# Transposes of a mixture-of-experts stage moved from TensorE to transposing DMAs on the SyncE queue

## The reference, cut to what matters

```
xn = rms_norm(layernorm(x))
scores = einsum('bsd,ed->bse', xn, w_router)          # 8 experts
ids = top 2 of scores; c = softmax(scores) at ids
h = einsum('bsd,ehd->bseh', xn, w_up)                 # 2 * 704 columns
val, gate = split(h, 2);  h = val * silu(gate)        # 704
y = einsum('bseh,edh->bsed', h, w_down)               # back to 256
out = sum over the 2 chosen experts of y * c, + xn input (skip)
```

## Time and profile before

| | us |
|---|---|
| three runs, median (lowest to highest) | 480.11 (479.94 to 484.15) |
| profiled execution, its own time | 481.64 |
| span of its one core | 479.8 |
| TensorE busy | 389.6 (81%) |
| VectorE busy | 278.7 (58%) |
| ScalarE busy | 260.5 (54%) |
| GpSimd busy | 196.5 (41%) |

### The profile page before, as it was taken

One profiled execution on the slowest core, in us unless ns is written; L12 is line 12 of the kernel. 1 busy time (PEld: TensorE's weight loads), 2 busy tenths in 40 slices (PEclk: granted clock), 3 DMA queues, 4 the chain that ended last, 5 costly groups with the idle time before them and its releaser, 6 DMA issues.

```text
span 479.8 us, 10289 instructions
## 1 busy us (share of the span) xinstructions
PE 389.6 (81%) x2600; PEld 272.6 (57%) x2601; DVE 278.7 (58%) x704; ACT 260.5 (54%) x473; POOL 196.5 (41%) x186
## 2 busy tenths in 40 slices
PE   1898897899984411059999999999999999999980
PEld 1676686788774311025666666666666666666660
DVE  4787677888883779854444444454444444444540
ACT  2898856745466750654555555555545555455530
POOL 2534535667774422112333344343344333344221
PEclk9999999799996555569999999999999999999997
DMA  7967991222261124001212222222222212222221
GB/s 250 376 244 252 382 313 48 66 68 67 66 216 46 45 59 122 23 14 32 46 36 44 44 44 33 41 38 44 44 44 33 43 35 44 44 44 33 35 24 11
DMA packets 24645, 41.93 MB, mean 87 GB/s; under 512 B 5040, under 2 KB 20400, under 8 KB 23600
## 3 DMA queue, kind: packets, MB, share of 16 engines
q1 hardware_dynamic: 17088, 31.17, 19.4%
q0 software_dynamic: 7536, 10.52, 13.8%
HBM read 32.17 MB, written 9.50 MB: 87 GB/s over the span
## 4 chain that ended last, share of the span: by engine, by line
PE 66%; DMA 10%; DVE 9%; ACT 5%; issue 4%; POOL 2%; SPq 2%; ACTq 0%; DVEq 0%; POOLq 0%
PE bank L1232 30%; DMA expert_w<-in_wup 6%; PE bank L1253 5%; PE bank L1283 4%; PE bank L1282 4%; PE bank L1284 4%; PE bank L1119 3%; DVE expert_w L931 3%; PE bank L1171 3%; DMA arena<-in_ctxT 2%; ACT arena L435 2%; PE bank L1180 2%; PE bank L1152 2%; PE bank L1264 2%; PE bank L1286 2%
## 5 line engine op out<-in xcount | busy, mean ns | idle before, releaser
L1232 PE MATMUL bank<-expert_w,arena 128*128 x702 | 160.4, 366 | 11.4 <-ACT arena L627 11.4
L741 POOL DMA_INDIRECT out<-arena,add_idx x39 | 61.7, 1581 | 115.9 <-ACT arena L608 115.9
L1232 PEld LDWEIGHTS bank<-expert_w,arena 128*128 128x128 f16 x702 | 62.9, 99 | 65.4 <-issue 14.8
L1051 DVE SCALAR_TENSOR_TENSOR arena<-bank,dn_small,arena 128x512 f32<-128x512 f32 x78 | 45.3, 581 | 39.2 <-PE bank L1232 24.0
L731 POOL DMA_INDIRECT arena<-xrow_hbm,take_idx x39 | 38.7, 993 | 67.5 <-PE bank L1264 46.2
L1282 PE MATMUL bank<-expert_w,arena 128*128 x195 | 53.2, 273 | 0.9 <-DVE arena L1035 0.9
L1283 PE MATMUL bank<-expert_w,arena 128*128 x195 | 53.2, 273 | 0.0
L1284 PE MATMUL bank<-expert_w,arena 128*128 x195 | 53.2, 273 | 0.0
L1035 DVE COPY arena<-bank 128x1024 f16<-128x1024 f16 x39 | 27.0, 691 | 42.3 <-PE bank L1253 42.3
L627 ACT ACTIVATE arena<-bank 128x512 f16<-128x512 f16 x39 | 23.3, 596 | 39.6 <-PE bank L1264 39.6
L1057 DVE TENSOR_TENSOR arena<-arena 128x512 f16<-128x512 f32 x39 | 27.0, 692 | 27.1 <-ACT arena L633 27.1
(11 more groups left out here) (181 smaller groups left out, 740.1 us busy)
## 6 DMA issues: line engine op xcount, KB each, us to landing
expert_w<-in_wup SPq DMA_DIRECT2D x8, 1408.0 KB, 7.3
expert_w<-in_wdn SPq DMA_DIRECT2D x10, 640.0 KB, 9.1
rows<-in_x SPq DMA_DIRECT2D x8, 256.0 KB, 6.8
arena<-in_ctxT SPq DMA_DIRECT2D x8, 256.0 KB, 4.6
xrow_hbm<-front SPq DMA_DIRECT2D x8, 256.0 KB, 2.2
out<-rows SPq DMA_DIRECT2D x8, 256.0 KB, 2.5
expert_w<-in_wdn SPq DMA_DIRECT2D x20, 64.0 KB, 9.0
cst_b<-in_consts_b SPq DMA_DIRECT2D x1, 960.0 KB, 7.8
```

Source lines behind the costliest of these rows:

```text
L741: pool.indirect_dma_start(out=out, in_=yt[:, i % 2], in_offset=None, out_offset=bass.IndirectOffsetOnAxis(ap=add_idx[:, i:i + 1], axis=0), ...
L1051: V.scalar_tensor_tensor(out=hh[:, cols], in0=src, scalar=h_scale[:, ds(e, 1)], in1=sg[:, cols], op0=ALU.mult, op1=ALU.mult).then_inc(s_h, 1)
L1232: last = T.matmul(bank[q][:, 0:n], xsT[:, slot, (2 * a + c) * P:(2 * a + c + 1) * P], up_w[:, ds(w0 + c * UPC + w * 2 * H + lo, n)], start ...
```

## The change

The transposes of the gathered rows and of h leave TensorE. SyncE issues a transposing DMA from SBUF to SBUF for each: one of 4 blocks of 128x128 fp16 for the rows (128 KB) and one of 11 blocks for `hs` (352 KB), 39 times each. The PSUM banks that held transposes become a second set for the up projection (banks 0 to 2 and 3 to 5) and for y (6 and 7); `hs` and `hT` get two buffers. The down projection of a slot moves one step later (step i + 3), and GpSimd issues four takes ahead in place of five. The last down matmul runs over 128 rows in place of 64. `tile_e` and others of the small tiles move to other places of the same buffer.

```diff
+            def step_e(it, k, r):                                    # @block.sync
+                if live(r, 2, NSLOT):
+                    i, half, slot = at(it, k, 2)
+                    sp.wait_ge(s_hhi, 2 * i + 2)
+                    sp.wait_ge(s_hlo, 2 * i + 2)
+                    if r >= 4:
+                        sp.wait_ge(s_y, i - 1)
+                    sp.dma_start_transpose(hT[:, slot], hs[:, slot]).then_inc(s_hT[slot], 16)
+                if live(r, 0, NSLOT):
+                    i, half, slot = at(it, k, 0)
+                    sp.wait_ge(s_xs[slot], 16 * half + 16)
+                    if r >= 2:
+                        sp.wait_ge(s_up, 3 * i - 3)
+                    sp.dma_start_transpose(xsT[:, slot], xs[:, slot, 0:4 * P]).then_inc(s_xsT[slot], 16)
+            steps(sp, step_e, E_STEPS[0], E_STEPS[0], E_STEPS[0])
...
@@ block.scalar: silu and high part of slot r-1 first, then yt of slot r-3
-                    nc.scalar.activation(hT[:, 8:NHS], hT_bank[1], ACT.Copy).then_inc(s_hTb, 1)
...
-                    nc.scalar.activation(xsT[:, slot], rowsT_bank, ACT.Copy).then_inc(s_xsT, 1)
...
+                    nc.scalar.activation(yt[:, slot], bank[6 + slot][:, 0:D], ACT.Copy, scale=pair_scale[:, ds(i, 1)]).then_inc(s_yt, 1)
...
@@ block.gpsimd
                 if i >= 2:
-                    pool.wait_ge(s_trx, i - 1)
+                    pool.wait_ge(s_xsT[i % 2], 16 * (i // 2))
                     pool.wait_ge(s_ps, i - 1)
...
-            for i in range(5):
+            for i in range(4):
                 take(i)
...
-                if i + 5 < NSLOT:
-                    take(i + 5)
+                if i + 4 < NSLOT:
+                    take(i + 4)
...
@@ block.vector: low part of slot r-1 first, then pair_scale of slot r
-                    V.tensor_copy(hT[:, 0:8], hT_bank[0]).then_inc(s_hTa, 1)
...
@@ block.tensor
+                if live(r, 1, NSLOT):
+                    i, half, slot = at(it, k, 1)
                     w_up = pe.snap(pe.value_load(tile_e[0:1, ds(i, 1)], min_val=0, max_val=NE - 1) * (2 * UPC))
+                    pe.wait_ge(s_xsT[slot], 16 * half + 16)
+                    for q, (lo, n) in enumerate(((0, HA), (HA, HA), (2 * HA, 2 * HB))):
+                        if r >= 3 and q != 1:
+                            pe.wait_ge(s_h, 2 * i - 3 + q // 2)
...
-                    for c in range(NHS):
-                        last = T.transpose(hT_bank[c // 8][:, c % 8], hs[:, c * P:(c + 1) * P], ident16[:, :])
-                    last.then_inc(s_trh, 1)
...
-                    for n in range(4):
-                        last = T.transpose(rowsT_bank[:, n * P:(n + 1) * P], xs[:, slot, n * P:(n + 1) * P], ident16[:, :])
-                    last.then_inc(s_trx, 1)
...
+                if live(r, 3, NSLOT):
+                    i, half, slot = at(it, k, 3)
                     w_dn = pe.snap(pe.value_load(tile_e[0:1, ds(i, 1)], min_val=0, max_val=NE - 1) * (2 * DNC))
+                    pe.wait_ge(s_hT[slot], 16 * half + 16)
+                    if r >= 5:
+                        pe.wait_ge(s_yt, i - 1)
```

More of the change, by code:

```diff
@@ L310, in steps @@
                 step(t // 2, t % 2, t)
-            with eng.Fori(lo // 2, hi // 2) as it:
-                step(it, 0, lo)
-                step(it, 1, lo + 1)
+            if hi > lo:
+                with eng.Fori(lo // 2, hi // 2) as it:
+                    step(it, 0, lo)
+                    step(it, 1, lo + 1)
             for t in range(hi, n):
@@ L1029, in step_e @@
             def step_e(it, k, r):
[L1030 to L1034, removed]
-                    V.tensor_copy(hT[:, 0:8], hT_bank[0]).then_inc(s_hTa, 1)
-                if live(r, 0, NSLOT):
-                    i, half, slot = at(it, k, 0)
-                    e = dve.snap(dve.value_load(tile_e[0:1, ds(i, 1)], min_val=0, max_val=NE - 1))
[L1039 to L1046, removed]
+                if live(r, 1, NSLOT):
+                    i, half, slot = at(it, k, 1)
+                    e = dve.snap(dve.value_load(tile_e[0:1, ds(i, 1)], min_val=0, max_val=NE - 1))
+                    up = bank[3 * slot:3 * slot + 3]
+                    for q, (src, cols) in enumerate(((up[1][:, 0:HA], slice(0, HA)), (up[2][:, HB:2 * HB], slice(HA, H)))):
                         dve.wait_ge(s_sg, 2 * i + q + 1)
@@ L1228, in _ @@
             products = [(c, a, w) for c in range(2) for a, w in ((0, 0), (0, 1), (1, 0))]
[L1230 to L1235, removed]
@@ L1266, in step_e @@
[L1266 to L1269, removed]
-                    up(i, slot, w_up, 2, 2 * HA, 2 * HB)
-                if live(r, 2, NSLOT):
-                    i, _, _ = at(it, k, 2)
+                    pe.wait_ge(s_xsT[slot], 16 * half + 16)
+                    for q, (lo, n) in enumerate(((0, HA), (HA, HA), (2 * HA, 2 * HB))):
+                        if r >= 3 and q != 1:
+                            pe.wait_ge(s_h, 2 * i - 3 + q // 2)
+                        for m, (c, a, w) in enumerate(products):
+                            last = T.matmul(bank[3 * slot + q][:, 0:n], xsT[:, slot, 2 * a + c],
+                                            up_w[:, ds(w_up + c * UPC + w * 2 * H + lo, n)],
+                                            start=m == 0, stop=m == len(products) - 1)
+                        last.then_inc(s_up, 1)
@@ L1281, in step_e @@
-                    for c in range(NH - 1):
-                        T.matmul(y, hT[:, c], dn_at(w_dn, c, 0), start=c == 0, stop=False)
-                        T.matmul(y, hT[:, c], dn_at(w_dn, c, 1), start=False, stop=False)
-                        T.matmul(y, hT[:, NH if c == NH - 2 else NH + 1 + c], dn_at(w_dn, c, 0), start=False, stop=False)
-                    T.matmul(y, hT[:, NH - 1], dn_at(w_dn, NH - 1, 0), start=False, stop=False)
-                    T.matmul(y, hT[0:HLAST, NH - 1], dn_at(w_dn, NH - 1, 1, HLAST), start=False, stop=True).then_inc(s_y, 1)
+                    pe.wait_ge(s_hT[slot], 16 * half + 16)
@@ new lines, in step_e @@
+                    if r >= 5:
+                        pe.wait_ge(s_yt, i - 1)
+                    y = bank[6 + slot][:, 0:D]
+                    for c in range(NH - 1):
+                        T.matmul(y, hT[:, slot, c], dn_at(w_dn, c, 0), start=c == 0, stop=False)
+                        T.matmul(y, hT[:, slot, c], dn_at(w_dn, c, 1), start=False, stop=False)
+                        T.matmul(y, hT[:, slot, NH if c == NH - 2 else NH + 1 + c], dn_at(w_dn, c, 0), start=False, stop=False)
+                    T.matmul(y, hT[:, slot, NH - 1], dn_at(w_dn, NH - 1, 0), start=False, stop=False)
@@ L1288, in _ @@
+                    T.matmul(y, hT[:, slot, NH - 1], dn_at(w_dn, NH - 1, 1), start=False, stop=True).then_inc(s_y, 1)
             steps(pe, step_e, *E_STEPS)
```

119 lines of the change are left out of this document (42 added, 77 removed).

## The result

The changed kernel takes 546.67 us at the median of five runs (537.92 to 550.1), the kernel before 480.6 (479.94 to 484.15) beside it: slower, by a ratio of 1.124 with a 95% interval of 1.115 to 1.133. The interval rests on its two runs of 537.92 and 544.49, since the other three, with a lower granted clock on TensorE (0.858 against 0.874 in the profiled one), are set apart. The profiled execution took 537.92, 56.3 more than that of before.

The account below looks back on a forecast made before the run. TensorE bounded the kernel before; afterwards the gather loop would. y(0) at 226, 18 pairs of 11.36 + 2.5 and 6.9 put y(38) at 482.4, +14.1: 495.7 profiled, 494.2 less 1.5 to the median; range 467 to 524.

Parts of the forecast that it names:

- What bounds the kernel, and what is removed: Stage E: TensorE bounds at 6.53 us a slot; without transposes its own work is 5.56 us.
- rival 2: TensorE stays the bound in stage E: a slot costs 5.56 us, the time is 451; chance 0.09.
- The loop through the gather: From y(i) through scaling, scatter, take, gather and rows' transposing DMA to up(i+4): binds, as take(i+4) stands behind scatter(i).
- 11.36 + T: Two slots' cost in us: 5.8 of scaling, scatter, take, gather and reactions, TensorE's 5.56, and T.
- T: Transposing DMA of the rows, in the wait for up(i+4): 2.2 plus 0.3, so 2.5 us.
- the 0.3 allowed: Added to the rows' transposing DMA for contention on the 16 DMA engines, where h's 352 KB may still be moving.
- The queue of SyncE: The rows' transpose stands behind h(i+2)'s, issued about 0.8 us after y(i); rows land in SBUF at 5.5, so no delay.
- H: Time SyncE is held by issuing h's 11-block transpose; claimed to cost nothing up to some 4.7 us.
- Rival 3: Transposing DMAs are slow and SyncE's queue binds: two slots cost 20.8 us, time near 633; chance 0.15.
- The end: After the last slots: y(38) ends 6.9 us after y(36), then the last scatter follows as before.
- Rivals 1 and 2: Rival 1: same gather loop, cheap transposes of 1.1 to 1.72 us, time 469 to 480, chance 0.23; rival 2 as above.
- 18 T - 30.9: Whole kernel's difference in us over 18 pairs of slots; nothing gained or lost at T = 1.72.

Follow-up runs that it names:

- five takes: The changed kernel with five takes ahead in place of four, h's transpose still issued first: 484.73 us, 1.004 of the kernel before.
- Filling the idle time: The changed kernel with 14 extra matmuls on TensorE ahead of each wait for the transposed rows: 516.41 us, 1.068 of the kernel before.
- the short h: The changed kernel with only 4 of h's 11 blocks transposed by the DMA (work left out, for times alone): 528.88 us, median of four runs.
- rows first: The changed kernel, four takes, with SyncE issuing the transpose of rows(r) ahead of that of h(r-2): 516.93 us, 1.076 of the kernel before.
- the kernel with rows first and six takes: The changed kernel with SyncE issuing the rows' transpose ahead of h's and six takes ahead: 449.98 us, 0.934 of the kernel before.

## Why the prediction was wrong

The direction and the mechanism were right, the size was not: 494.2 forecast, at most 524, and 546.67 measured. By the ends of the down projections of the profiled executions, the 56.3 us more are:

| step of the prediction | forecast | measured | differs by |
|---|---|---|---|
| start: y(0) ends at | 226 | 227.34 | +1.3 |
| pair of slots, mean of 18 | 13.86 | 15.95 | +37.6 |
| y(36) to y(38) | 6.9 | 6.51 | -0.4 |
| y(38) to the last scatter | as before, 0.81 | 4.37 | +3.6 |

which with the 14.1 forecast makes 56.2.

- *What bounds the kernel, and what is removed.* Right: once the waits are out of the way a slot takes 5.4 to 5.7 us, and the kernel comes to 450, which is what rival 2 gave for a free TensorE.
- *The loop through the gather.* Right in each link, shown by the trace in order of time and by the take's place: five takes remove 62 us. The step that failed is its sum, "two slots cost 11.36 + T", with T = 2.5. T itself was right (2.4). Two terms were missing or short. In the two slots shown, TensorE's part of the loop is 7.18 us (346.83 to 354.01) where 5.56 were forecast, and the rest 9.04 (354.01 to 363.05) where 5.8 + 2.5 = 8.3 were. **The clock**: the 5.56 us of TensorE in the loop were taken at the full clock. The loop lets TensorE idle, and behind 12 pieces of idle time (2.2 to 5.0 us long) in the 18 pairs the up projection, which lies on the loop, runs partly at 1.2 GHz. Filling the idle time shows the price, 15.95 against 14.72, 1.2 us a pair or 22 us in all. I had written down the piece of idle time as a thing the profile would show, used the half clock for the start, and did not ask what it would cost inside. **Contention and order**: against the 0.3 allowed stand 0.7 on the gather (3.5 for 2.8) and 0.2 on T (2.4 for 2.2), and ScalarE starts on y 0.27 and 0.68 us after its end in the two slots shown, not 0.04, since the change put L640 behind the high part of h. That makes 0.8 to 1.2 us a pair, and 14.72 - 13.86 = 0.9 is left when the clock is full, 15 us in all. What the gather, T and ScalarE each have of it is read from the trace; only the gather's part was tried, by the short h and by rows first, and ScalarE's order was not.
- *The price of T.* Landing after 2.4 us, within 0.1 of the estimate of 2.35 by the Trainium skill, Advanced Engine Details and Errata, section X-Bar Transpose (TRN2). The trace does not bear out the rate given there, 350 to 400 GB/s: seven blocks more (224 KB) cost 1.1 to 1.2 us, some 200 GB/s, so the 2.4 us are mostly the fixed part. Behind h's transpose it is 4.6 us, however, which no part of the prediction had.
- *The queue of SyncE.* H costs nothing in the changed kernel, as forecast: L427 holds SyncE for 1.4 us. (h is whole 6.5 us into the step, not 6.1.) But the prediction took the queue's order to matter only through SyncE being held; a DMA behind h's is held up longer, 4.6 us to landing in place of 2.4. The five-take run shows that this second loop, 12.9 us, lies right behind the first. Rival 3's mechanism was real and its size much smaller: 11 blocks land in 3.5 us at least and 4 in 2.4, so the blocks of one DMA don't run one after the other at 1.31 us each, the figure for one block in the Trainium skill, VectorE: DVE Perf Modes, section The three transpose paths.
- *The end.* "What follows is the last scatter, as before" failed: y(36), y(37) and y(38) come close together, and each scatter waits for the landing of the one before (4.4 to 4.6 us).
- *Rivals 1 and 2* fell for this kernel. Rival 2's 451 is what the kernel with rows first and six takes reaches (449.98).
- *Chances.* The bound of "within 1%" was put at the wrong T: by 18 T - 30.9, 4.8 us are reached at T = 1.98, not 2.25. It has no part in the miss.

## What to carry to other kernels

When work leaves the busiest engine, follow the loop that will bind next through every in-order queue, and cost TensorE's part of it also at the lower clock that it may get after idling, not only at the clock of the saturated kernel. A prefetch is only as early as its place on the queue: two more takes ahead and an exchange of two steps on SyncE's queue turned 547 us into 450. Where two transfers share the DMA engines, put the urgent one ahead of the long one: how long the issue of the long one takes (1.4 us here) doesn't show how much later the one behind it lands (2.2 us).

## What the runs showed of the hardware

- Extra matmuls made a kernel faster by 30 us (22 profiled): 546 of them, in idle time behind which the clock had fallen in 12 of 36 steps.
- The length of one piece of idle time didn't tell whether TensorE's clock would fall: 3.64 us left it at 1.00 and 2.18 us brought 0.68 over the up projection behind.
- While transposing DMAs and a gather ran together, the profile shows the DMA engines as busy throughout (a share of 1.13 and 1.18, the number before the last, so full) at some 200 GB/s:

```profile
348.00:349.00 1.00, 1.00 (x4) 0.36 (x3) 0.00 (x0) 0.00 (x0) 0.00 (x0) 0.50 1.13 186
349.00:350.00 1.00, 1.00 (x4) 0.40 (x3) 0.00 (x0) 0.21 (x1) 0.00 (x0) 0.50 1.18 214
```

- Transposing DMAs move packets of 256 bytes. The hardware queue shows 94464 packets in place of 17088; 39 x 15 blocks x 128 rows of 256 bytes are 74880, and 32 more for each of the 78 DMAs make exactly the difference, 77376. They land in 2.4 us for 4 blocks and 3.5 at the least for 11, so the seven blocks more cost 1.1 to 1.2 (3.6 is the median where five takes run ahead).
- They hold SyncE for 1.19 us (4 blocks) and 1.26 to 1.40 (11 blocks), while a plain store's issue takes some 0.4. One behind the other, the second lands in 4.6 us in place of 2.4.
